# Keeping the attention output in SBUF between two stages of a transformer layer, and two block ends without GpSimd's drain

## Chip, cores and metric

One Trainium2 chip. The kernel runs on 8 cores, one sequence of the batch on each, with no exchange between them. Cores 0 to 3 lie on one die, 4 to 7 on the other. The metric is the device time of one execution in microseconds (us), that of the slowest core.

## The reference

A layer of a transformer, post-norm, for 8 sequences of 2048 tokens and width 2048. The attention is over features: the scores are a 2048 × 2048 matrix of feature against feature. The FFN has 8192 hidden units and ternary weights, which are made from the float weights inside the computation.

```python
q = einsum('bse,ef->bsf', x, Wq); k = ...Wk; v = ...Wv
scores = einsum('bes,bfs->bef', qT, kT) / sqrt(64)      # E x E per sequence
attn   = softmax(scores, axis=-1)
o      = einsum('bef,bfs->bes', attn, vT)               # E x S
x = layernorm(x + einsum('bse,ef->bsf', swap(o), Wo))
w_q = sign(w) * (abs(w) >= 0.7 * mean(abs(w)))          # for w1 and w2
h = gelu(einsum('bsd,fd->bsf', x, w1_q) + b1)
x = layernorm(x + einsum('bsf,df->bsd', h, w2_q) + b2)
```

## The kernel before

Sizes: P = 128 partitions, S = E = 2048 (16 row blocks each), FF = 8192 (64 row blocks). Every matmul takes a 128 × 128 left operand and 512 columns in bf16. Each stage is one block with a program for each engine, and a barrier of all engines stands at a block's end. A block has the drain of GpSimd in front of that barrier, unless it is made with `no_gpsimd_drain=True`. Here `p2`, `p3`, `f1`, `f2` are, `p1` and `p4` are not.

- **p1** (to about 928 us): mean of |w1| and |w2| on ScalarE; q, k, v on TensorE. q and v are spilled to `q_h` and `v_h` in HBM, k stays in `big1`. At the end GpSimd issues the loads of the first half of Wo into `wbuf` (two DMAs, which cast f32 to bf16); they are needed in `p4`.
- **p2** (to about 1226 us): first the thresholds on VectorE, a small matmul that spreads them (L484), then for each of 16 blocks the scores in `psS` from `qsl`, a slice loaded from `q_h` in pieces of 256 bytes, by SP, two blocks ahead. SP issues the first only when all q and v spills have landed. The softmax numerators go to `big0`, row block e at `big0[:, e*S : e*S+S]`, the reciprocals of the row sums to `recip_all`.
- **p3** (1226 to 1591 us): for each row block e_m TensorE transposes the 16 tiles of `big0` row block e_m into `psTA` or `psTB`, ScalarE copies them to `atsl` (L658), TensorE multiplies `atsl` by v in `big1` into `psO` (L635, 64 matmuls). ScalarE evacuates `psO` times the reciprocal to the staging tile `ostg` (L663), waits for that evacuation and stores it to `o_h` in HBM. `psO` and `atsl` exist once, so evacuation, copy and the next matmuls come one after the other. TensorE issues the transposes of the next row block ahead of the wait for the evacuation.
- **p4** (1591 to 2062 us): for each of 16 token blocks s_m SP loads `osl`, the columns of that block from all of `o_h`, again in pieces of 256 bytes, two buffers. TensorE makes the 128 × 2048 block of o·Wo (L749): 32 matmuls with `wbuf`, then 32 with `wobuf2`, the second half of Wo, which GpSimd loads at the stage's start. VectorE adds the residual `xres` to it in four pieces (L783) and, after ScalarE has made the statistics and the square root, applies the layer norm to `x2t` (L799). ScalarE casts to `x2b` (L857) and stores to `x2_h`. TensorE transposes `x2b` three blocks later into `psT4` (L732), and ScalarE copies this to `big0` (L812), column block pm of every row block: this is the left and moving side of the FFN. TensorE starts block s_m only when VectorE has done two pieces of the block before.
- **Quantizing** runs beside `p2`, `p3`, `p4` and `f1`: 256 tiles of w1 and w2, in pairs. GpSimd loads a pair to `qin` when VectorE is done with the pair before (`emit_quant_loads`, L216). VectorE makes two masks (L225, L228) and their difference in `qout` (L236), for which the spill of the pair before must have landed. SP spills a pair to `w1q_h` or `w2q_h` (`emit_quant_spills`, L208). `qin` and `qout` exist once, so a pair's round trip is a chain of a load, VectorE and a store. In `p4`, 3 tiles stand in VectorE's program in each token block, one before the statistics are waited for and two after. SP's program interleaves the spills with the `osl` loads; before `osl` of block s_m it waits for TensorE to finish block s_m − 2 (`t_y`).
- **f1** (2071 to 2963 us): h = gelu(x·w1), 64 row blocks of 64 matmuls (L911), weight slices `w1sl` loaded by SP from `w1q_h`; the 128 tiles of w2 are quantized beside it. **f2** (from 2963 us): h·w2, residual, layer norm, output.

Of the kernel before, what the change touches and what calls it, by code (L numbers as in the profile page):

```python
# [6 lines left out]
BF16 = mybir.dt.bfloat16  # L7
# [4 lines left out]
P = 128  # L12
S = 2048
E = 2048
# [64 lines left out]
def build_nc(upto=6, debug=False):  # L79
# [21 lines left out]
    o_h = nc.dram_tensor("o_h", [E, S], BF16, kind=scratch_kind)  # L101
# [8 lines left out]
    with contextlib.ExitStack() as stx:  # L110
# [66 lines left out]
        with nc.sbuf_tensor("big0", [P, nE * S], BF16) as big0, \  # L177
# [64 lines left out]
            with nc.sbuf_tensor("big1", [P, nE * S], BF16) as big1:  # L242

                with nc.psum_tensor("psA", [P, 2048], F32) as psA, \
# [3 lines left out]
                     nc.Block("p1") as blk:  # L248
# [348 lines left out]
                if upto >= 3:  # L597
                    with nc.psum_tensor("psO", [P, 2048], F32) as psO, \
# [3 lines left out]
                         nc.sbuf_tensor("ostg", [P, 2 * 2048], BF16) as ostg, \  # L602
# [48 lines left out]
                        def _(s):  # L651
                            s.wait_ge(v_rc.h, 16)
                            for e_m in range(nE):
# [7 lines left out]
                                if e_m >= 2:  # L661
                                    c_o.wait_item(s, e_m - 2)
                                s.activation(ostg[:, (e_m % 2) * 2048:  # L663
                                                  (e_m % 2) * 2048 + 2048],
# [4 lines left out]
                                s.wait_ge(a_oev.h, e_m + 1)  # L669
                                c_o.issue(s, hap(o_h, e_m * P * S, [[S, P], [1, S]]),  # L670
                                          ostg[:, (e_m % 2) * 2048:
                                               (e_m % 2) * 2048 + 2048])

            if upto >= 4:
                QT4_LO = QT_P2 + QT_P3
                with nc.psum_tensor("psy0", [P, 512], F32) as psy0, \
# [6 lines left out]
                     nc.sbuf_tensor("osl", [P, 2 * 2048], BF16) as osl, \  # L683
# [4 lines left out]
                     nc.Block("p4") as blk:  # L688
# [20 lines left out]
                    def _(sy):  # L709
                        c_o.wait_all(sy)  # L710
                        for s_m in range(nS):
                            if s_m >= 2:
                                sy.wait_ge(t_y.h, s_m - 1)
                            s_osl.issue(
                                sy, osl[:, (s_m % 2) * 2048:(s_m % 2) * 2048 + 2048],
                                hap(o_h, s_m * P, [[S, P], [P * S, nE], [1, P]]))
                            emit_quant_spills(
                                sy, QT4_LO + (s_m * (QT_W1 - QT4_LO)) // nS)
# [3 lines left out]
                    def _(t):  # L722
# [15 lines left out]
                        psy = [psy0, psy1, psy2, psy3, psy4, psy5]  # L738
                        for s_m in range(nS):
                            s_osl.wait_item(t, s_m)  # L740
                            if s_m >= 1:
                                t.wait_ge(v_z.h, max(0, 4 * s_m - 2))
                            for e_k in range(nE):
# [4 lines left out]
                                for nb in range(4):  # L748
                                    mm = t.matmul(  # L749
                                        psy[(4 * s_m + nb) % 6][:],  # L750
                                        osl[:, (s_m % 2) * 2048 + e_k * P:
                                            (s_m % 2) * 2048 + e_k * P + P],
# [52 lines left out]
                    def _(s):  # L805
# [4 lines left out]
                        def x2fm_evacs(pm):  # L810
                            s.wait_ge(t_tr4.h, pm + 1)
# [366 lines left out]
```

## Time and profile before

| | us |
|---|---|
| two runs | 3947.11 and 4346.39, median 4146.75 |
| the profiled execution | 3943.83 |
| span of its slowest core (core 1) | 3942.3 |
| spans of the 8 cores | 3898.1 to 3942.3 |
| granted TensorE clock, mean, each core | 0.925 to 0.927 |

The page of the profile, by engine and by slice of the span (40 slices, 98.6 us each; a digit is a busy share in tenths):

```profile
PE 3238.6 (82%) x14917; PEld 1457.3 (37%) x14917; DVE 1256.4 (32%) x1362; ACT 740.1 (19%) x1065; POOL 92.6 (2%) x166
PE   0986899835985877466649999999997999989997
DMA  9899966874345545566646777776656333372232
```

PE is TensorE, PEld its weight loads, DVE VectorE, ACT ScalarE, POOL GpSimd, SP SyncE; a q behind a name is the engine's own instruction queue, which issues DMAs. TensorE is the busiest by far, and its slices show where it isn't: `p1`'s start, its end (slice 9), and slices 16 to 20, which are the end of `p3` and `p4`. The idle time before an instruction stands in brackets in the timelines, with what ended it.

### The profile page before, as it was taken

What the parts mean: (1) busy time and instruction counts of PE and PEld (TensorE: products, weight loads), DVE (VectorE), ACT (ScalarE), POOL (GpSimd) and SP (SyncE); (2) the same over time, 40 slices, a digit from 0 to 9 for tenths busy, and PEclk for the clock granted to TensorE, in tenths of its full rate; (3) what the DMA queues carried; (4) which work ended last, traced back from release to release, by engine and by line L of the source; (5) the groups of instructions that cost most, each with busy time, mean ns of one, the idle gap of its engine ahead of it and who ended that gap; (6) DMA issues with size and microseconds to landing.
All of it is one profiled execution on the core that took longest, in us unless ns stands there. A gap on an engine that the chain in (4) does not pass through costs nothing. (4 is left out here: it accounts for less than half of the span.)

```text
span 3942.3 us, 37616 instructions; the slowest of 8 cores (3898.1 to 3942.3 us)
## 1 busy us (share of the span) xinstructions
PE 3238.6 (82%) x14917; PEld 1457.3 (37%) x14917; DVE 1256.4 (32%) x1362; ACT 740.1 (19%) x1065; POOL 92.6 (2%) x166
## 2 busy tenths in 40 slices
PE   0986899835985877466649999999997999989997
PEld 0432344312432333122224444444442444434443
DVE  0111211101443444144434334343431333323333
ACT  1344433340111111123331111111110000200002
POOL 0000000000000000000000000000000000000000
PEclk9998999967997989787779999999998999999998
DMA  9899966874345545566646777776656333372232
GB/s 186 214 249 252 241 171 176 231 218 94 100 111 177 164 155 157 126 203 202 192 155 182 187 187 187 187 203 190 194 171 218 128 128 115 132 244 81 112 128 86
DMA packets 392943, 673.62 MB, mean 171 GB/s; under 512 B 210432, under 2 KB 267840, under 8 KB 368192
## 3 DMA queue, kind: packets, MB, share of 16 engines
q1 hardware_dynamic: 291216, 377.55, 31.3%
q0 software_dynamic: 41648, 184.60, 19.8%
q10 hardware_dynamic: 59904, 109.06, 7.7%
q8 instruction: 119, 1.95, 0.2%
q14 instruction: 56, 0.46, 0.0%
HBM read 545.37 MB, written 159.38 MB: 179 GB/s over the span
## 5 line engine op out<-in xcount | busy, mean ns | idle before, releaser
L911 PE MATMUL psH<-big,w1sl 128*128 128x512 bf16 x4096 | 887.2, 379 | 14.0 <-DMA w1sl<-w1q_h 14.0
L1005 PE MATMUL psF<-w2g,hg 128*128 128x512 bf16 x4096 | 890.8, 380 | 0.0
L911 PEld LDWEIGHTS psH<-big,w1sl 128*128 128x128 bf16 x4096 | 400.4, 98 | 500.4 <-issue 20.7
L1005 PEld LDWEIGHTS psF<-w2g,hg 128*128 128x128 bf16 x4096 | 400.4, 98 | 490.1 <-issue 13.0
L225 DVE TENSOR_SCALAR qmask<-qin,tbc 128x1024 f32<-128x1024 f32 x256 | 208.0, 812 | 777.3 <-DMA qin<-w2t 475.5
L1055 DVE TENSOR_TENSOR oacc<-psF,oacc 128x2048 f32<-128x2048 f32 x112 | 256.6, 2292 | 583.1 <-PE psF L1005 583.1
L430 ACT ACTIVATE qmask<-sbin 128x1024 f32<-128x1024 f32 x256 | 270.3, 1056 | 484.1 <-DMA sbin<-w1t 212.7
L236 DVE TENSOR_TENSOR qout<-qmask 128x1024 bf16<-128x1024 f32 x256 | 313.7, 1226 | 135.2 <-DMA w1q_h<-qout 60.3
L635 PE MATMUL psO<-big,atsl 128*128 128x512 bf16 x1024 | 248.5, 408 | 91.8 <-ACT atsl L658 65.2
L299 PE MATMUL psA<-wbuf,big 128*128 128x512 bf16 x1024 | 228.7, 385 | 111.0 <-DMA wbuf<-wq 98.2
L299 PE MATMUL psB<-wbuf,big 128*128 128x512 bf16 x1024 | 231.4, 388 | 49.1 <-DVE spillb L345 49.1
L928 ACT ACTIVATE hstg<-psH,b1sb 128x2048 bf16<-128x2048 f32 x64 | 126.0, 1969 | 751.6 <-PE psH L911 751.6
L497 PE MATMUL psS<-big,qsl 128*128 128x512 bf16 x1024 | 231.5, 389 | 18.7 <-DMA qsl<-q_h 18.7
L749 PE MATMUL psy<-wbuf,osl 128*128 128x512 bf16 x512 | 133.8, 427 | 127.3 <-DMA osl<-o_h 113.2
L228 DVE TENSOR_SCALAR qmask<-qin,tbc 128x1024 f32<-128x1024 f32 x256 | 206.5, 807 | 0.0
L635 PEld LDWEIGHTS psO<-big,atsl 128*128 128x128 bf16 x1024 | 104.9, 104 | 230.3 <-issue 127.6
L299 PEld LDWEIGHTS psA<-wbuf,big 128*128 128x128 bf16 x1024 | 101.1, 99 | 236.1 <-issue 119.1
L314 PE MATMUL psA<-big,wbuf 128*128 128x512 bf16 x512 | 113.8, 384 | 74.9 <-ACT wbuf L409 74.9
L299 PEld LDWEIGHTS psB<-wbuf,big 128*128 128x128 bf16 x1024 | 101.7, 100 | 176.9 <-issue 61.8
L497 PEld LDWEIGHTS psS<-big,qsl 128*128 128x128 bf16 x1024 | 101.4, 100 | 148.3 <-issue 35.0
L749 PEld LDWEIGHTS psy<-wbuf,osl 128*128 128x128 bf16 x512 | 53.8, 107 | 204.1 <-issue 159.5
L314 PE MATMUL psB<-big,wbuf 128*128 128x512 bf16 x512 | 111.8, 379 | 6.7 <-ACT wbuf L409 6.7
(107 smaller groups left out, 1150.5 us busy)
## 6 DMA issues: line engine op xcount, KB each, us to landing
sbin<-w1t SPq DMA_DIRECT2D x128, 512.0 KB, 6.2
sbin<-w2t SPq DMA_DIRECT2D x128, 512.0 KB, 5.8
qin<-w1t POOLq DMA_DIRECT2D x64, 1024.0 KB, 6.3
qin<-w2t POOLq DMA_DIRECT2D x64, 1024.0 KB, 7.7
w2g<-w2q_h SPq DMA_DIRECT2D x16, 4096.0 KB, 14.1
w1q_h<-qout SPq DMA_DIRECT2D x64, 512.0 KB, 7.2
w1sl<-w1q_h SPq DMA_DIRECT2D x64, 512.0 KB, 10.7
w2q_h<-qout SPq DMA_DIRECT2D x64, 512.0 KB, 9.0
```

The costliest lines, as they stand in the source:

```text
L225: v.tensor_scalar(qmask[:], src, tbc[:, 4 * j:4 * j + 1], tbc[:, 4 * j + 1:4 * j + 2], op0=ALU.subtract, op1=ALU.is_ge)
L228: v.tensor_scalar(qmask2[:], src, tbc[:, 4 * j + 2:4 * j + 3], tbc[:, 4 * j + 3:4 * j + 4], op0=ALU.subtract, op1=ALU.is_le).then_inc(g_qm ...
L236: v.tensor_tensor(qout[:, (i % 2) * 1024:(i % 2) * 1024 + 1024], qmask[:], qmask2[:], op=ALU.subtract).then_inc(v_qt.h, 1)
L299: mm = t.matmul(pv, big0[:, e_k * S + s_m * P:e_k * S + s_m * P + P], half[:, e_k * 512:e_k * 512 + 512], start=(e_k == 0), stop=(e_k == n ...
L314: mm = t.matmul(ps[:, sn * 512:sn * 512 + 512], wbuf[:, (f_m % 8) * 2048 + e_k * P: (f_m % 8) * 2048 + e_k * P + P], big0[:, e_k * S + sn ...
L430: s.activation(sink[:], sbin[:, (i % 3) * 1024:(i % 3) * 1024 + 1024], AF.Abs, accum_out=stats_acc[:, i:i + 1]).then_inc(a_st.h, 1)
L497: mm = t.matmul(ps[:, nb * 512:nb * 512 + 512], qsl[:, (e % 2) * 2048 + s_k * P: (e % 2) * 2048 + s_k * P + P], big1[:, s_k * S + nb * 512 ...
L635: mm = t.matmul(psO[:, sn * 512:sn * 512 + 512], atsl[:, f_k * P:f_k * P + P], big1[:, f_k * S + sn * 512: f_k * S + sn * 512 + 512], star ...
L749: mm = t.matmul(psy[(4 * s_m + nb) % 6][:], osl[:, (s_m % 2) * 2048 + e_k * P: (s_m % 2) * 2048 + e_k * P + P], wsrc[:, wof + nb * 512:wof ...
L911: mm = t.matmul(ps[:, nb * 512:nb * 512 + 512], w1sl[:, (f_m % 2) * 2048 + d_k * P: (f_m % 2) * 2048 + d_k * P + P], big0[:, d_k * S + nb ...
L1005: mm = t.matmul(ps[:, nb * 512:nb * 512 + 512], hg[:, slot * 8192 + f_k * 1024 + j * P: slot * 8192 + f_k * 1024 + j * P + P], w2g[:, slot ...
L1055: v.tensor_tensor(oacc[:, j * 2048:j * 2048 + 2048], ps[:], oacc[:, j * 2048:j * 2048 + 2048], op=ALU.add).then_inc(v_fa.h, 1)
```

## The change

Four edits, of which two belong together:

1. `p3` writes the evacuated attention output over `big0`, row block e_m, whose transposes have been read by then, instead of to `ostg`. The store to `o_h`, the wait ahead of it and the tensor `o_h` go. A wait of ScalarE for the transposes of its own row block is added.
2. `p4` takes its left operand from `big0` at `big0[:, e_k*S + s_m*P : +P]`. The `osl` loads and their waits go, as does SP's wait on `t_y` that paced them. TensorE waits once for the last evacuation of `p3`. ScalarE's copy L812, which writes into the same columns, gets a wait for TensorE to be done with that token block.
3. `p1` and 4. `p4` are made with `no_gpsimd_drain=True`.

```diff
-                     nc.Block("p1") as blk:
+                     nc.Block("p1", no_gpsimd_drain=True) as blk:
...
                                 s.wait_ge(t_o.h, e_m + 1)
-                                if e_m >= 2:
-                                    c_o.wait_item(s, e_m - 2)
-                                s.activation(ostg[:, (e_m % 2) * 2048:
-                                                  (e_m % 2) * 2048 + 2048],
+                                s.wait_ge(t_tr.h, e_m + 1)
+                                s.activation(big0[:, e_m * S:e_m * S + S],
                                              psO[:], AF.Copy,
                                              scale=recip_all[:, e_m:e_m + 1]
                                              ).then_inc(a_oev.h, 1)
                                 a_oev.inc(1)
-                                s.wait_ge(a_oev.h, e_m + 1)
-                                c_o.issue(s, hap(o_h, e_m * P * S, [[S, P], [1, S]]),
-                                          ostg[:, (e_m % 2) * 2048:
-                                               (e_m % 2) * 2048 + 2048])
...
-                     nc.Block("p4") as blk:
+                     nc.Block("p4", no_gpsimd_drain=True) as blk:
...
                     def _(sy):
-                        c_o.wait_all(sy)
                         for s_m in range(nS):
-                            if s_m >= 2:
-                                sy.wait_ge(t_y.h, s_m - 1)
-                            s_osl.issue(
-                                sy, osl[:, (s_m % 2) * 2048:(s_m % 2) * 2048 + 2048],
-                                hap(o_h, s_m * P, [[S, P], [P * S, nE], [1, P]]))
                             emit_quant_spills(
                                 sy, QT4_LO + (s_m * (QT_W1 - QT4_LO)) // nS)
...
+                        t.wait_ge(a_oev.h, nE)
                         for s_m in range(nS):
-                            s_osl.wait_item(t, s_m)
                             if s_m >= 1:
                                 t.wait_ge(v_z.h, max(0, 4 * s_m - 2))
...
                                         psy[(4 * s_m + nb) % 6][:],
-                                        osl[:, (s_m % 2) * 2048 + e_k * P:
-                                            (s_m % 2) * 2048 + e_k * P + P],
+                                        big0[:, e_k * S + s_m * P:e_k * S + s_m * P + P],
...
                             s.wait_ge(t_tr4.h, pm + 1)
+                            s.wait_ge(t_y.h, pm + 1)
                             s.copy(bass.AP(big0, pm * P, [[nE * S, P], [S, nE], [1, P]]),
```

## Rows read from the trace of the kernel before

**Rows 1.** The page of the profile, its first line.

```profile
span 3942.3 us, 37616 instructions; the slowest of 8 cores (3898.1 to 3942.3 us)
```

**Rows 2.** Busy time by stretch (p4's middle, f1); then clock, DMA share, GB/s.

```profile
1722.00:1824.00 102.00, 66.63 (x320) 31.19 (x320) 48.14 (x77) 32.80 (x60) 5.25 (x10) 0.80 0.63 196
...
2071.00:2963.00 892.00, 886.72 (x4096) 400.27 (x4094) 353.08 (x384) 125.34 (x64) 33.31 (x63) 1.00 0.67 186
```

**Rows 3.** Groups of instructions, 1592 to 2062 us: busy, mean ns | idle before, releasers.

```profile
L749 PE MATMUL psy<-wbuf,osl 128*128 128x512 bf16 x512 | 133.8, 427 | 127.3 <-DMA osl<-o_h 113.2 <-DVE x2t L783 14.1
```

**Rows 4.** Timeline around the end of p1: start, duration, instructions [idle before].

```profile
911.37 14.14 ACTq L58 DMA_DIRECT2D v_h<-spillb  x2
...
923.20 1.49 POOL L58 DMA_DIRECT2D wbuf<-wo  x2 [415.43 <-PE psB L314]
...
954.04 0.36 DVE L512 TENSOR_SCALAR thw<-tvals 1x1 f32<-1x1 f32 x2 [26.65 <-PEq L248]
...
966.30 44.04 PE L497 MATMUL psS<-big,qsl 128*128 128x512 bf16 x191
```

**Rows 5.** DMA issues at p1's end and p2's start: count, KB, us to landing.

```profile
wbuf<-wo POOLq DMA_DIRECT2D x1, 2048.0 KB, 29.4
...
v_h<-spillb ACTq DMA_DIRECT2D x1, 512.0 KB, 9.8
...
qsl<-q_h SPq DMA_DIRECT2D x3, 512.0 KB, 4.8
```

**Rows 6.** Timeline of p3, one row block; the last row is from p1.

```profile
1298.07 1.97 ACT L663 ACTIVATE ostg<-psO,recip_all 128x2048 bf16<-128x2048 f32 x1 [16.39 <-PE psO L635]
...
1300.59 1.87 ACT L658 COPY atsl<-psTA 128x2048 bf16<-128x2048 bf16 x1 [0.55 <-ACT ostg L663]
...
1303.17 15.45 PE L635 MATMUL psO<-big,atsl 128*128 128x512 bf16 x64 [4.30 <-ACT atsl L658]
...
272.49 15.38 PE L299 MATMUL psB<-wbuf,big 128*128 128x512 bf16 x64 [3.02 <-DVE spillb L345]
```

**Rows 7.** DMAs at p4's start: issue, landing times, and queues from 1600 to 1630.

```profile
1592.36 1.55 POOL L58 DMA_DIRECT2D wobuf<-wo  x2
...
wobuf<-wo POOLq DMA_DIRECT2D x1, 2048.0 KB, 30.3
...
osl<-o_h SPq DMA_DIRECT2D x1, 512.0 KB, 39.0
...
q0 software_dynamic: 1273, 6.45, 93.6%
q1 hardware_dynamic: 1381, 0.35, 7.4%
```

**Rows 8.** Timeline of p4's start.

```profile
1632.54 9.40 PE L749 MATMUL psy<-wbuf,osl 128*128 128x512 bf16 x32 [44.11 <-DMA osl<-o_h]
...
1649.04 0.69 DVE L783 SCALAR_TENSOR_TENSOR x2t<-psy,xres 128x512 f32<-128x512 f32 x1 [73.45 <-PE psy L749]
```

**Rows 9.** Timeline of p4, two token blocks (a cycle).

```profile
1720.73 0.69 DVE L783 SCALAR_TENSOR_TENSOR x2t<-psy,xres 128x512 f32<-128x512 f32 x1 [5.63 <-PE psy L749]
...
1752.53 1.23 DVE L236 TENSOR_TENSOR qout<-qmask 128x1024 bf16<-128x1024 f32 x1 [4.68 <-DMA w1q_h<-qout]
...
1754.86 9.67 PE L749 MATMUL psy<-wbuf,osl 128*128 128x512 bf16 x32 [8.60 <-DMA osl<-o_h]
...
1771.82 0.69 DVE L783 SCALAR_TENSOR_TENSOR x2t<-psy,xres 128x512 f32<-128x512 f32 x1 [5.06 <-PE psy L749]
```

**Rows 10.** Landing of a spill in that cycle, with and without an osl load beside it.

```profile
w1q_h<-qout SPq DMA_DIRECT2D x1, 512.0 KB, 13.2
...
w1q_h<-qout SPq DMA_DIRECT2D x1, 512.0 KB, 8.6
```

**Rows 11.** The chain of work in f1, two spills in a row: start, duration.

```profile
2102.14 9.15 DMA w2q_h<-qout
...
2115.72 8.36 DMA w2q_h<-qout
```

More of the change, by code:

```diff
@@ L100, in build_nc @@
     v_h = nc.dram_tensor("v_h", [E, S], BF16, kind=scratch_kind)
-    o_h = nc.dram_tensor("o_h", [E, S], BF16, kind=scratch_kind)
     x2_h = nc.dram_tensor("x2_h", [S, E], F32, kind=scratch_kind)
@@ L601, in build_nc @@
                          nc.sbuf_tensor("atsl", [P, 2048], BF16) as atsl, \
-                         nc.sbuf_tensor("ostg", [P, 2 * 2048], BF16) as ostg, \
                          nc.Block("p3", no_gpsimd_drain=True) as blk:
@@ L682, in build_nc @@
                      nc.psum_tensor("psT4", [P, 2048], BF16) as psT4, \
-                     nc.sbuf_tensor("osl", [P, 2 * 2048], BF16) as osl, \
                      nc.sbuf_tensor("xres", [P, 2 * 2048], F32) as xres, \
```

## The prediction

> **What bounds the kernel now.** I read first the busy time by stage, then what ended the idle time of TensorE in the stages that the diff touches, then those stretches in order of time. The profiled execution spans 3942.3 us [rows 1] and took 3943.8 us as a whole; the sum below is made against 3943.8. The median of the two runs shown (4146.75) is the mean of 3947.11 and 4346.39. The profiled time agrees with the lower one within 0.1%, so I forecast against that level.
>
> The last two stages (`f1`, `f2`, from 2071 on) hold nearly half of the time and nothing in the diff enters them. In `f1` TensorE is busy 886.7 of 892 us [rows 2]. They will move as a block, earlier by what the stages before them give. In `p4` TensorE is far from full: its 512 matmuls on the first half of Wo alone waited 113.2 us for `osl<-o_h`, the tile that the change abolishes, against 14.1 us for VectorE [rows 3]. 44.1 us of that is one wait [rows 8] at the start of `p4`; the other 69.1 us are seven waits, one in every second row block from the third on. The question is what each of these waits hides. What removing a wait is worth is what comes second, not the wait.
>
> **Part 1, the block end of `p1`.** GpSimd issues the two Wo loads at 923.20. VectorE is then idle 26.65 us until 954.04, at the block's end barrier [rows 4]. The second, issued about 923.95, lands 29.4 us later [rows 5], at 953.3, 0.7 us ahead of the release. So I read the 26 us as the drain waiting for these loads, and with `no_gpsimd_drain` the barrier opens at about 928.5. It is not all gained: the loads still have to land, and three things come between.
> - SP waits for the last `v_h` spill. The last store of the two, issued about 925.2, lands 9.8 us later [rows 4, 5], so the first `qsl` load can't leave before 935.
> - The threshold chain on VectorE and the small matmul behind it take 966.3 − 954.0 = 12.3 us [rows 4] and would be over at 941, so they are no longer last.
> - `qsl` then shares the DMA engines with Wo. A `qsl` load takes 4.8 us alone [rows 5]. The nearest row for it in competition is the first `osl` load, of the same shape and also right behind two Wo loads: it landed 39.0 us after issue, while the second Wo load had landed at 1593.14 + 30.3 = 1623.4 and `osl` only at 1632.5 [rows 7, 8].
>
> Bounds: if the engines gave `qsl` half of their time, it would land at 935.3 + 2 × 4.8 = 945, a gain of 966.3 − 945 = 21. If all that is queued goes ahead (Wo until 953.3, two `qsl` loads 9.6, the first `qin` 3 to 5), it lands at 966 to 968, a gain of nothing or a loss of 2. I take a landing 8 us behind Wo, about what `osl` shows: 961, **a gain of 5**.
>
> The Trainium skill, DMA: Bandwidth & Descriptors, section on queues, rings and completion order, says that an engine takes turns between its queues packet by packet. The rows agree: from 1600 to 1630 SP's queue moved 1381 packets beside 1273 of GpSimd's [rows 7], which is turn by turn. By that rule `qsl` (2048 small packets) can't be through before Wo's remaining 4 KB packets are, so about 957 would be its earliest, a gain of at most 9.
>
> The same flag on `p4` I cost at nothing: GpSimd's last load there landed long before the last piece of ScalarE work.
>
> **Part 2, the loop of `p3`.** For each of the 16 row blocks ScalarE evacuates `psO`, waits for its own evacuation, issues the `o_h` store, then copies the next transposed tile, and TensorE waits for that copy (4.30 us of idle time) [rows 6]. Evacuation to copy takes 1300.59 − 1298.07 = 2.52 us, of which 1.97 is the evacuation and 0.55 idle [rows 6]. The destination changes from `ostg` to `big0`, with the same shape and type, so 1.97 stays; the new wait on `t_tr` was met before the copy and costs nothing. The 0.55 to 0.65 go, 15 times on the path (the last is the next part's): **a gain of 9**, bounds 7 and 10. The 16 stores are off TensorE's path here, and I count no more for them. TensorE's gap shrinks to 3.7 us, which won't spare its slow start: after a gap of 3.02 us 64 matmuls took 15.38 us [rows 6], as after 4.30.
>
> **Part 3, the start of `p4`.** Before, TensorE waits 44.11 us for `osl` and starts at 1632.54; the first residual add is at 1649.04 [rows 8]. After, the left operand is already in `big0`, so the first 32 matmuls start at once, and then wait for the second half of Wo (`wobuf2`). This is the new wait. It landed at 1623.4. Without `osl` beside it, it should land earlier by its share: SP's queue held 7.4% of the engines [rows 7], 2.2 of 30 us, and 0.4 us come from the store no longer issued, so 1620.8. The 32 matmuls behind it take 9.4 us with a slow start, as the first 32 do now [rows 8], and the add starts at 1630.3: **a gain of 19**. Bounds: 16 if the landing doesn't move, 21 if it moves by a whole `osl` load.
>
> **Part 4, the steady part of `p4`.** Two row blocks take 1771.82 − 1720.73 = 51.1 us [rows 9], a cycle that repeats six times after it has begun. In one block of the two the `osl` load leaves together with `qin`, `xres`, the `x2_h` store and the spill of quantized weights. There the spill lands 13.2 us after its issue, in the other block 8.6 [rows 10]. This delays two chains:
> - TensorE starts at 1754.86 after 8.60 us of waiting for `osl` [rows 9], so it could start at 1746.3, held there by the transposes. It then ends at 1762.8 instead of 1771.4.
> - VectorE, quantizing in between, writes at 1752.53 after waiting 4.68 us for the spill [rows 9]. The pieces behind that leave it free 5.06 us before the next add at 1771.82 [rows 9], at 1766.7. So even with an unchanged spill the cycle gives 5.1.
>
> Without `osl` the burst loses 4.8 of about 15 us of DMA work. Between 8.6 and 13.2 I take 10.0 for the spill, the lower end plus a bit for the `x2_h` store that the other block doesn't have. VectorE is then free 3.2 us earlier, at 1763.5, or 1763.1 with `qin` a little faster too. So both chains meet at about 1763, and the new bound is the quantizing chain on VectorE and its two DMAs: 8.7 us per cycle. There are seven such waits: 7 × 8.7 = **a gain of 61**. Bounds: 7 × 5.1 = 36 with the spill at 13.2, and 7 × 9.2 = 65 with it at 8.6, where TensorE is last. SP's spills no longer stand behind the `t_y` wait; this gives nothing, since they were issued right after their tile. DMA share is 0.63 here [rows 2], so bandwidth isn't the next bound. The added `t_y` wait of ScalarE is met a few row blocks before: zero.
>
> **Sum.** 5 + 9 + 19 + 61 = 94, and 3943.8 − 94 = **3850 us**, 2.4% less.
>
> **Rivals.**
> - *The spill stays slow* (13 us because of `qin`, `xres` and `x2_h`, not of `osl`). For it speaks that three megabyte-sized transfers stay in that burst; against it that the other block lands in 8.6 with two of them. It gives 5 + 9 + 19 + 36 = 69: 3875 us. Chance 0.17.
> - *Everything at the good end*: `qsl` gets through early, the latencies of all DMAs in `p4` fall. 21 + 10 + 21 + 65 = 117: 3827 us. Against it stands the late `osl` landing. Chance 0.08.
> - *Slower: quantizing takes over `f1`.* There each pair of tiles goes round in 2115.72 − 2102.14 = 13.6 us [rows 11], while TensorE needs 892/64 = 13.9 per slice; the weights for the next stages come from that loop, and the spills share SP's queue with TensorE's `w1sl` loads. If the pair grows by 1.8 us it adds 64 × 1.5 = 96 us and the whole gain is gone; at 3.0 us more it adds 173 and the kernel is at 4023. Against it: nothing in `f1` is changed, and its DMA traffic stays. Chance 0.04.
> - *The flag doesn't lift the 26 us*, because the barrier waits for something else. It costs only the 5 of part 1: 3855, within the forecast's own range.
>
> **Chances and range.** The forecast has 0.71, with its own range of 3833 to 3873. 2% of the time, about what a measurement can tell from no change, is 79 us, so the boundary lies at 3865, between the forecast and the first rival. Of the forecast's 0.71 I put 0.05 above the boundary, where the spill is between 11 and 13. Faster: 0.66 + 0.08 = 0.74. Within 2%: 0.17 + 0.05 = 0.22. Slower: 0.04. The range for 8 in 10 takes in the upper half of the good rival and the first rival with a little spread: 3820 to 3880.
>
> **What would show it.** Part 1: after the last `p1` work, SP and VectorE resume within 1 us, and the first L497 matmul is at 957 to 966 in the old time. Part 2: ScalarE's copy follows the evacuation without the 0.55 us, and TensorE's gap is 3.7. Part 3: TensorE starts at the block's start, then waits some 15 us for `wobuf<-wo`. Part 4: no `osl`; two row blocks take 42 to 43 us, with idle time of VectorE on `qin` and the spill as the largest rest. `f1` keeps its 892 us, and `f1` and `f2` together their 3942 − 2071 = 1871. The forecast is wrong if the cycle stays above 46 us (the spill), or `f1` gets longer by more than 10 us.

## The result, and the profile after

The changed kernel takes 0.9774 of the time of the kernel before, with a 95% interval of 0.9749 to 0.9799: 2.3% less. Its lowest execution took 3849.17 us (before: 3944.47 in the same session), and the profiled one 3859.17 (before: 3943.83). Executions of either kernel in which the cores of a die show a lower granted clock take 4 to 12% longer (one of the two runs behind the median of 4146.75 is such a one), so everything below compares undisturbed executions or, where a profile shows one die disturbed, cores 4 to 7 of the other.

The page of the kernel after (the span of its slowest core, core 2, then busy time, then slices as before):

```profile
span 3857.6 us, 37557 instructions; the slowest of 8 cores (3821.2 to 3857.6 us)
PE 3236.5 (84%) x14917; PEld 1456.7 (38%) x14917; DVE 1255.9 (33%) x1362; ACT 736.9 (19%) x1065; POOL 92.6 (2%) x166
PE   0987899926984888677759999999988999989997
DMA  9899965875345444555647766777547233462232
```

TensorE is busy for as long as before; only idle time has gone. Where, a table by stretch shows. Each number is worked out from the first and last starts of one line's instructions on each core, as the mean of the eight cores (L635 is the matmul of `p3`, in the kernel after at L633):

| stretch, us | before | after | difference | forecast |
|---|---|---|---|---|
| start to the last value matmul of `p1` | 918.5 | 920.2 | +1.7 | 0 |
| from there to the first score matmul | 43.6 | 37.2 | −6.4 | −5 |
| `p2`, first to last score matmul | 247.7 | 248.4 | +0.7 | 0 |
| from there to the first matmul of `p3` | 44.6 | 45.1 | +0.5 | 0 |
| `p3`, first to last L635 | 327.7 | 315.3 | −12.4 | −9 |
| from there to the first residual add of `p4` | 59.2 | 39.5 | −19.7 | −19 |
| `p4`, first to last residual add | 377.8 | 333.2 | −44.6 | −61 |
| from there to `f1` | 41.5 | 40.8 | −0.7 | 0 |
| `f1`, first to last matmul | 887.5 | 888.6 | +1.1 | 0 |
| from there to the end | 975.8 | 974.1 | −1.7 | 0 |

Together −81.5 us in the mean span of the cores in these two profiled executions (3923.9 to 3842.4), where the forecast's parts add up to −94. The ratio of all undisturbed executions, which takes the slowest core of each, makes it 89. Three of the four parts came out within 4 us. The steady part of `p4` gave 45 and not 61.

**The end of `p1`.** Timeline of the kernel after, its slowest core; it answers to [rows 4]:

```profile
920.82 1.49 POOL L58 DMA_DIRECT2D wbuf<-wo  x2 [417.91 <-PE psB L313]
...
925.44 0.15 ACT L445 COPY tvals<-psA 1x4 f32<-1x4 f32 x1 [27.86 <-PE psA L324]
...
933.63 41.15 SPq L58 DMA_DIRECT2D qsl<-q_h  x3
...
937.83 0.56 PE L483 MATMUL psS<-tq,ones_f 1*128 1x8 f32 x2 [12.48 <-DVE thw L550]
...
958.36 41.88 PE L496 MATMUL psS<-big,qsl 128*128 128x512 bf16 x184 [19.96 <-DMA qsl<-q_h]
```

The barrier is open at once: VectorE goes on at 926, SP issues at 933.63, when the last v spill has landed, and the threshold chain is over at 938. Then TensorE waits 19.96 us for `qsl`. The two DMAs, by the time from issue to landing:

```profile
wbuf<-wo POOLq DMA_DIRECT2D x1, 2048.0 KB, 32.3
...
qsl<-q_h SPq DMA_DIRECT2D x1, 512.0 KB, 24.6
```

The second Wo load lands at about 921.6 + 32.3 = 953.9 (29.4 us after issue before, [rows 5], now slowed by `qsl`), and `qsl` at 958.2, 4 us behind it.

**`p3`.** Timeline from one row block into the next, to be read beside [rows 6]:

```profile
1295.78 15.66 PE L633 MATMUL psO<-big,atsl 128*128 128x512 bf16 x64 [3.66 <-ACT atsl L656]
...
1311.60 1.97 ACT L660 ACTIVATE big<-psO,recip_all 128x2048 bf16<-128x2048 f32 x1 [16.49 <-PE psO L633]
1313.46 1.86 ACT L656 COPY atsl<-psTB 128x2048 bf16<-128x2048 bf16 x1
...
1316.03 13.97 PE L633 MATMUL psO<-big,atsl 128*128 128x512 bf16 x64 [3.69 <-ACT atsl L656]
```

Evacuation to copy takes 1.86 us instead of 2.52, and the gap is 3.7 us, as forecast. What the forecast excluded is the last row: in 2 of the 15 row blocks that follow a gap (3 on two of the eight cores) the 64 matmuls took 13.97 us, with no slow start. The granted clock was 1.00 in the first 3 us of that block and 0.69 in those of the block at 1295.78.

**The start of `p4`**, beside [rows 7, 8]:

```profile
1577.44 8.44 PE L734 MATMUL psy<-wbuf,big 128*128 128x512 bf16 x32 [6.33 <-DMA b2bf<-b]
1604.73 8.45 PE L734 MATMUL psy<-wobuf,big 128*128 128x512 bf16 x32 [18.85 <-DMA wobuf<-wo]
1613.38 0.69 DVE L767 SCALAR_TENSOR_TENSOR x2t<-psy,xres 128x512 f32<-128x512 f32 x1 [53.19 <-PE psy L734]
```

The new wait is where it was expected, for the second half of Wo. A small one for `b2bf` stands before it and costs nothing behind the larger one. On the mean of the eight cores (below: the mean core) the second load of `wobuf` lands 25.5 us after its issue, where it took 28.0 beside `osl`.

**The steady part of `p4`**, one cycle of two token blocks, beside [rows 9]: VectorE's tile behind a spill, TensorE's first half, VectorE's first residual add.

```profile
1736.00 1.23 DVE L235 TENSOR_TENSOR qout<-qmask 128x1024 bf16<-128x1024 f32 x1 [2.46 <-DMA w1q_h<-qout]
...
1743.32 0.69 DVE L767 SCALAR_TENSOR_TENSOR x2t<-psy,xres 128x512 f32<-128x512 f32 x1 [1.79 <-PE psy L734]
...
1752.08 1.23 DVE L235 TENSOR_TENSOR qout<-qmask 128x1024 bf16<-128x1024 f32 x1 [4.73 <-DMA w1q_h<-qout]
...
1765.59 0.69 DVE L767 SCALAR_TENSOR_TENSOR x2t<-psy,xres 128x512 f32<-128x512 f32 x1
...
1787.39 0.69 DVE L767 SCALAR_TENSOR_TENSOR x2t<-psy,xres 128x512 f32<-128x512 f32 x1 [1.83 <-PE psy L734]
```

The cycle is 1787.39 − 1743.32 = 44.1 us where I had 42.4 and the kernel before 51.1. The `osl` waits are gone and VectorE's wait for the spill is as long as it was (4.73 against 4.68 us). The same holds for the whole steady part, here on core 2 (what waited for what, us in total, times, the longest):

```profile
DVE qmask L224 <- DMA qin<-w1t: 58.8, 18, 5.2
...
DVE qout L235 <- DMA w1q_h<-qout: 53.2, 19, 5.1
```

On the mean core VectorE waits there 64 us for loads of tiles, 51 for spills and 5 for TensorE; before it was 89, 51 and 32. So VectorE and the DMAs of its tiles are what `p4` waits for now, as the prediction said they would be.

The landing times of that spill and its neighbour, beside [rows 10]:

```profile
w1q_h<-qout SPq DMA_DIRECT2D x1, 512.0 KB, 11.6
...
w1q_h<-qout SPq DMA_DIRECT2D x1, 512.0 KB, 8.7
```

### The profile page after: what moved, and what is told of

Read it like the earlier page. It is cut to its first block and busy times, and to the rows that moved or that the text cites. A ratio compares the mean times of both kernels' runs of the same rounds, so it can differ in the third digit from the quotient of the medians.

```text
span 3857.6 us, 37557 instructions; the slowest of 8 cores (3821.2 to 3857.6 us)
## 1 busy us (share of the span) xinstructions
PE 3236.5 (84%) x14917; PEld 1456.7 (38%) x14917; DVE 1255.9 (33%) x1362; ACT 736.9 (19%) x1065; POOL 92.6 (2%) x166
## 5 line engine op out<-in xcount | busy, mean ns | idle before, releaser
L633 PE MATMUL psO<-big,atsl 128*128 128x512 bf16 x1024 | 247.7, 407 | 83.7 <-ACT atsl L656 55.3
L496 PE MATMUL psS<-big,qsl 128*128 128x512 bf16 x1024 | 228.2, 385 | 41.5 <-DMA qsl<-q_h 41.5
L633 PEld LDWEIGHTS psO<-big,atsl 128*128 128x128 bf16 x1024 | 105.0, 104 | 221.4 <-issue 118.2
L734 PE MATMUL psy<-wbuf,big 128*128 128x512 bf16 x512 | 130.1, 418 | 25.2 <-DVE x2t L767 18.9
L734 PE MATMUL psy<-wobuf,big 128*128 128x512 bf16 x512 | 114.5, 382 | 18.8 <-DMA wobuf<-wo 18.8
```

What stands on the lines that cost most here:

```text
L496: mm = t.matmul(ps[:, nb * 512:nb * 512 + 512], qsl[:, (e % 2) * 2048 + s_k * P: (e % 2) * 2048 + s_k * P + P], big1[:, s_k * S + nb * 512 ...
L633: mm = t.matmul(psO[:, sn * 512:sn * 512 + 512], atsl[:, f_k * P:f_k * P + P], big1[:, f_k * S + sn * 512: f_k * S + sn * 512 + 512], star ...
L734: mm = t.matmul(psy[(4 * s_m + nb) % 6][:], big0[:, e_k * S + s_m * P:e_k * S + s_m * P + P], wsrc[:, wof + nb * 512:wof + nb * 512 + 512] ...
```

## The experiments

All times by stretch are as in the table above, and "steady part" is the first to the last residual add of `p4`.

### 1. The flag of p1 alone

```diff
 # the kernel before
-                     nc.Block("p1") as blk:
+                     nc.Block("p1", no_gpsimd_drain=True) as blk:
```

> The kernel before with one edit: the block p1 is made without GpSimd's drain. Theory (the barrier waited for the two Wo loads, and what the barrier gives back is mostly lost to the same loads, which now run beside the first q slice): SP and VectorE go on within 1 us of the end of p1's work, the first score matmul starts about 37 us after the last matmul of p1's values instead of 43.6 (mean of the cores), the rest is unchanged, 3938 us, within 2%. Rival 1, the barrier waits for something else: the 43.6 us stay. Rival 2, the early start brings nothing at all: the stretch stays 43.6 although the barrier opens early. Both rivals: 3944 us.

Measured on cores 4 to 7: from the last value matmul to the first score matmul 36.2 us (before: 43.4). The barrier, in the timeline of core 5:

```profile
920.63 1.49 POOL L58 DMA_DIRECT2D wbuf<-wo  x2 [417.15 <-PE psB L314]
922.62 0.33 ACTq L58 DMA_DIRECT2D v_h<-spillb  x1
925.84 0.36 DVE L512 TENSOR_SCALAR thw<-tvals 1x1 f32<-1x1 f32 x2 [1.02 <-PEq L248]
```

VectorE goes on after 1.02 us, where it waited 26.65 [rows 4]. So the drain was the wait, and 7 us of the 26 are what one gets for it. That the drain waited for the Wo loads, the kernel before shows core by core: the second load lands 29.8 to 31.2 us after the last value matmul, and on each of the eight cores VectorE goes on 0.7 us behind that landing. As a whole no difference from the kernel before could be told by time alone.

### 2. The output in big0, with both drains back

```diff
 # the kernel after
-                     nc.Block("p1", no_gpsimd_drain=True) as blk:
+                     nc.Block("p1") as blk:
...
-                     nc.Block("p4", no_gpsimd_drain=True) as blk:
+                     nc.Block("p4") as blk:
```

> The changed kernel with the drain of GpSimd back at the ends of p1 and p4, so only the attention output stays in big0. Theory (three gains by place: 12 us in p3, 20 at the start of p4, 45 in its steady part, nothing at the end of p4): 3857 + 6 = 3863 us, about 2.1% less than before, the stretch from the last residual add of p4 to the first FFN matmul is 41 us with or without the drain. Rival (the flag at the end of p4 has a part in the gain): that stretch is longer by more than 2 us than in the changed kernel.

Measured: the end of `p1` is back at 43.5 us on cores 4 to 7, `p3` 315.6, steady part 333.3, and from the last add to `f1` 40.4 (after: 40.9). The flag on `p4` does nothing there. The gain of the rest hardly depends on the flags: only the first residual add of `p4` comes 1.7 us later after `p3` (41.6 against 39.9 us), with the second load of `wobuf` landing later.

### 3. The stores back in p3

```diff
 # the kernel after, p3, ScalarE, behind the evacuation
                                 a_oev.inc(1)
+                                s.wait_ge(a_oev.h, e_m + 1)
+                                c_o.issue(s, hap(o_h, e_m * P * S, [[S, P], [1, S]]),
+                                          big0[:, e_m * S:e_m * S + S])
```

> The changed kernel with the 16 stores of the attention output to o_h put back into p3, from big0, and ScalarE's wait for its own evacuation ahead of each; nothing reads o_h. The prediction had 0.6 us for each of 15 row blocks in p3 (9 us), the changed kernel showed 12.4. Theory 1 (wait and issue on ScalarE are all of it): the p3 stretch goes back from 315 to 327 us, p4 stays at 333 between its first and last residual add. Theory 2 (the rest of the 12.4 is less DMA traffic for the load of the values and for quantizing): the same, since the traffic is back as well, but then the first p3 matmul moves too. Rival (p3's gain came from the wait for the landing of older stores): the stretch stays near 318.

Measured on cores 4 to 7: `p3` 328.7 us (before 327.8, after 315.5), steady part 333.0. The whole gain of `p3` is the store with ScalarE's wait and issue; where the store reads from plays no part. The run puts the wait and the stores' DMA traffic back together and doesn't separate them. Two things speak for the wait: TensorE's gap is 4.3 us again where it was 3.7, and the first matmul of `p3`, which the second theory had move, doesn't come later (43.1 us after the last of `p2`, against 45.2). The evacuations in the kernel after come 20.2 us apart, and 18.5 in two or three of fifteen cases; before and here mostly 20.5 to 20.9, with one or two of 22. The forecast 9 is in the shorter gap, and two spared slow starts of 1.7 us make up the rest.

### 4. The osl traffic back, without its wait

```diff
 # the kernel after, p4, SyncE
                         for s_m in range(nS):
+                            if s_m >= 2:
+                                sy.wait_ge(t_y.h, s_m - 1)
+                                s_osl.wait_item(sy, s_m - 2)
+                            s_osl.issue(
+                                sy, osl[:, (s_m % 2) * 2048:(s_m % 2) * 2048 + 2048],
+                                hap(q_h, s_m * P, [[E, P], [P * E, nE], [1, P]]))
                             emit_quant_spills(
```

> The changed kernel with the 16 loads of 256-byte pieces put back on SP in p4 at their old places and with their old pacing, into a tile that nothing reads (they read q_h, which lies the same way as o_h did). TensorE waits for none of them. It tells the wait from the traffic. Theory (mine: without the traffic the spill of quantized weights lands in 10 instead of 13 us, which is a good part of the gain in p4): the steady part of p4 grows from 333 to about 350 us, and the first residual add moves 2 us later. Rival (the wait of TensorE was all that counted): 333 stays. Rival 2 (the pacing and the issue on SP's queue hold up the spills): over 360.

Measured: steady part 344.5 us over all cores (345.7 on cores 4 to 7), against 333.2 without the traffic and 377.8 with traffic and wait. So of the 44.6 us some 11 are traffic that spills and loads no longer share, and 33 are TensorE's wait. The rival that only the wait counts falls, and my price of the traffic (17) was too high. The first residual add comes 4 us later, not 2. The slow spill of each cycle shows why the traffic matters less than I had it: it lands in 12.7 to 13.2 us before (core 1), in 11.5 to 12.0 after and in 11.2 to 12.8 here (core 2).

### 5. The transposes in the middle of the next block

```diff
 # the kernel after, p4, TensorE
                                 if s_m == 0 and e_k == 8:
                                     g_wo2.wait_all(t)
+                                if s_m >= 4 and e_k == 8:
+                                    x2_transposes(s_m - 4)
...
-                            if s_m >= 3:
-                                x2_transposes(s_m - 3)
+                        x2_transposes(nS - 4)
                         x2_transposes(nS - 3)
```

> The changed kernel, in p4 the 16 transposes of an older token block are issued after the first 32 matmuls of the next block instead of ahead of them. In the changed kernel the blocks of p4 last 21.5 and 22.5 us in turn. Theory (the short one, which I had forecast at 19.6, is ended by a chain: layer norm, ScalarE's cast, its copy of psT4, the transposes that wait for it, then 64 matmuls with a slow start; the long one by the quantizing chain on VectorE): the short block falls to 19.6 to 20, the long one stays, so the steady part goes from 333 to about 320 us. Rival (both blocks are held by the quantizing chain): 333 stays. Rival 2 (the matmuls' own length decides): 333 stays too, with TensorE busy all through the block.

Measured: steady part 333.5 us, unchanged (ratio 0.9789, interval 0.9768 to 0.9810). The short block did as the theory said, but the sum is that of the first rival. The first residual adds of three token blocks in a row, on core 2:

```profile
1762.42 0.68 DVE L768 SCALAR_TENSOR_TENSOR x2t<-psy,xres 128x512 f32<-128x512 f32 x1
...
1782.27 0.68 DVE L768 SCALAR_TENSOR_TENSOR x2t<-psy,xres 128x512 f32<-128x512 f32 x1
...
1806.94 0.68 DVE L768 SCALAR_TENSOR_TENSOR x2t<-psy,xres 128x512 f32<-128x512 f32 x1
```

The short block is 19.8 us, as the theory had it, and the long one has grown to 24.7. Their sum is 44.5, as before the edit. Over the eight cores the seven long blocks grew by 8.0 us together and the eight others shrank by 7.7. TensorE waits for nothing but VectorE's residual adds in the steady part:

```profile
PE psy L736 <- DVE x2t L768: 84.6, 15, 11.1
```

VectorE in turn waits 0.1 us for TensorE on the mean core, 71 for loads of tiles and 51 for spills. So the quantizing chain sets the sum of two blocks, in which three pairs of tiles are quantized. The prediction's way of adding up the ends of single blocks falls here.

### 6. Two pairs of quantized tiles

```diff
 # the kernel after
-             nc.sbuf_tensor("qout", [P, 2 * 1024], BF16) as qout, \
+             nc.sbuf_tensor("qout", [P, 4 * 1024], BF16) as qout, \
...
-                    if i >= 2:
-                        c_wq.wait_item(v, i // 2 - 1)
+                    if i >= 4:
+                        c_wq.wait_item(v, i // 2 - 2)
```

> The changed kernel with room for two pairs of quantized tiles in qout, so a pair no longer waits for the landing of the spill just ahead of it, only for the one before that (the statistics buffers of p1 lie over it, for room). Theory (the long block of p4 is ended by the spill, which lands 11.6 to 12.0 us after its issue where I had forecast 10): the long block falls from 22.5 to about 20, the short one stays at 21.5, the steady part goes from 333 to about 315 us. Rival (the load of the next pair decides, the spill only came last by a hair): less than 5 us of gain. f1 stays at 886.

Measured: steady part 310.5 us, 23 less, and 0.972 of the kernel before (interval 0.9694 to 0.9746). VectorE in the same place, core 2:

```profile
1725.25 0.69 DVE L773 SCALAR_TENSOR_TENSOR x2t<-psy,xres 128x512 f32<-128x512 f32 x1 [3.35 <-PE psy L740]
...
1734.47 1.23 DVE L236 TENSOR_TENSOR qout<-qmask 128x1024 bf16<-128x1024 f32 x1 [0.17 <-DVE qmask L228]
1741.55 0.81 DVE L225 TENSOR_SCALAR qmask<-qin,tbc 128x1024 f32<-128x1024 f32 x1 [5.85 <-DMA qin<-w1t]
```

No wait for a spill is left on any core; the load of the next pair is what VectorE waits for now (67 us on the mean core). The tiles and their traffic are the same, so this is what the wait for the spill cost, and the rival of less than 5 us falls. The token blocks are 20.7 us on average.

### 7. Sixteen tiles moved from p4 to p2

```diff
 # the kernel after
-QT_P2 = 24
+QT_P2 = 40
```

> The changed kernel with 40 instead of 24 of the 256 tiles quantized in p2, so 32 instead of 48 are left for p4: two in each token block, one pair. Theory (the quantizing chain ends the long blocks of p4): without the long chain every block is ended by the transposes' chain or shorter, 20 us, and the steady part goes from 333 to about 305 us; p2 has 1.25 pairs of 11.7 us in each 14 us of matmuls, and its q loads stand behind the spills on SP, so it grows by 10 to 20 us. Sum: 3840 to 3850 us. Rival (p2 is ended by its spills from then on): p2 grows by more than p4 gives.

Measured: 0.9705 of the kernel before (interval 0.9674 to 0.9736). Its lowest execution took 3819.31 us, less than the 3840 to 3850 expected. Steady part 244.5 us, 89 less; `p2` 297.9, 50 more and not 10 to 20. The steady part fell much below the 305 that I expected, since with one pair in each block the round trip of 14 to 15 us fits inside what TensorE needs. TensorE in `p4`, on core 7:

```profile
1763.59 7.07 PE L734 MATMUL psy<-wbuf,big 128*128 128x512 bf16 x32
1770.50 7.07 PE L734 MATMUL psy<-wobuf,big 128*128 128x512 bf16 x32
1778.69 1.05 PE L717 MATMUL psT<-ident_bf,x2b 128*128 128x128 bf16 x16 [1.12 <-ACT big L797]
1779.58 7.07 PE L734 MATMUL psy<-wbuf,big 128*128 128x512 bf16 x32
```

Most blocks take 15.8 to 16.6 us, on average 16.3, and 64 matmuls take 14 us as at the full clock. VectorE now waits 50 us for TensorE and 1 for loads of tiles. So what bounds `p4` in the changed kernel isn't the transposes' chain but 1.5 round trips per block. The edit takes a third of the tiles' DMA traffic and of VectorE's work on them out of `p4` as well; of the 89 us, only the 23 of experiment 6 are shown with work and traffic unchanged.

The 50 us in `p2` are TensorE's waits for `qsl`, 56.5 us on the mean core where they were 19.6, and slower matmuls behind those gaps, 13 us. Lines of core 0:

```profile
1094.36 11.85 SPq L58 DMA_DIRECT2D w1q_h<-qout  x2
...
1106.30 0.39 SPq L58 DMA_DIRECT2D qsl<-q_h  x1
...
1115.03 15.15 PE L496 MATMUL psS<-big,qsl 128*128 128x512 bf16 x57 [10.12 <-DMA qsl<-q_h]
```

The load leaves right behind the second of two spills, which SP holds back until VectorE has made its tiles. So it is for all 14 later loads on all eight cores: each is issued 0.4 us behind a spill, on average 10.6 us after its buffer has come free (4.3 in the kernel after), and lands in 9.0 us (8.0). So, as far as the trace tells, it is the order on SP that costs the time, and the shared engines 1 us of each load. The expectation's rival holds as to the cause, but `p2` grew by less than `p4` gave.

### 8. The copy to atsl in halves

```diff
 # the kernel after, p3: ScalarE, then TensorE
-                                s.copy(atsl[:], pt[:]).then_inc(a_trs.h, 1)
+                                for hh in range(2):
+                                    s.copy(atsl[:, hh * 1024:hh * 1024 + 1024],
+                                           pt[:, hh * 1024:hh * 1024 + 1024]
+                                           ).then_inc(a_trs.h, 1)
...
-                                t.wait_ge(a_trs.h, e_m + 1)
+                                t.wait_ge(a_trs.h, 2 * e_m + 1)
...
+                                    if f_k == 8:
+                                        t.wait_ge(a_trs.h, 2 * e_m + 2)
```

> The changed kernel, in p3 ScalarE copies the transposed tiles to atsl in two halves, and TensorE starts after the first. Its gap in each of 15 row blocks should fall from 3.7 to 2.8 us. In the changed kernel two of the fifteen gaps of 3.69 us were followed by 64 matmuls in 13.97 us and the others by 15.66. Theory 1 (a gap under 3 us keeps the TensorE clock at 2.4 GHz, as 2.44 us did in p1): 15 x (0.9 + 1.7) = 39 us off the row blocks, but the quantizing of 28 pairs in p3 is over only 13 us before the stage's end and takes over, so the stage gives about 13 us and then stands. Rival (the clock falls all the same): 15 x 0.9 = 13 us, with 64 matmuls in 15.4 us.

Measured: 0.9759 of the kernel before (interval 0.9736 to 0.9783), so 6 us less than after by these ratios, whose intervals overlap, and 10 by the stretches of `p3` and its end. Three row blocks of `p3` on TensorE:

```profile
1349.69 13.97 PE L635 MATMUL psO<-big,atsl 128*128 128x512 bf16 x64 [2.84 <-ACT atsl L659]
...
1367.46 15.66 PE L635 MATMUL psO<-big,atsl 128*128 128x512 bf16 x64 [2.90 <-ACT atsl L659]
...
1386.82 13.97 PE L635 MATMUL psO<-big,atsl 128*128 128x512 bf16 x64 [2.81 <-ACT atsl L659]
```

With gaps of 2.8 to 2.9 us 9 or 10 of 15 row blocks on each core start at the full clock, where with 3.7 us it was 2 or 3. In the first 3 us of the three blocks above the granted clock was 1.00, 0.62 and 1.00. So neither the theory (all of them) nor the rival (none) holds. `p3` falls from 315 to 290 us, but from its last matmul to the first of `p4` it takes 20.6 instead of 6.1 us: the barrier waits for the quantizing of `p3`'s 28 pairs. As in `p4`, quantizing takes over.

### 9. Both quantizing edits together

```diff
 # the kernel after: QT_P2 = 40, and qout with two pairs as in experiment 6
```

> The two edits of qout_two_pairs and qt_p2_40 together: a second pair of qout, and 40 tiles quantized in p2. Theory (a pair's round trip, load, VectorE and spill, is what p4 and the longer p2 wait for, and both edits act on it): p4's steady part stays at the floor of 244 us that TensorE sets, p2 falls from 298 towards 280, since the spill leaves the round trip but the load stays; 3800 us. Rival (p2's 50 us came from the q loads behind the spills on SP): p2 stays at 298.

Measured: 0.9683 (0.9665 to 0.9701), the lowest execution 3803.35 us. `p2` 294.7 us instead of 297.9, steady part 240. The landing of the spill was not what held `p2`; taking it out of the round trip gave 3 us there and not the 18 that I expected. The rival holds: the loads of `qsl` still leave 0.4 us behind a spill, 10.4 us after their buffer has come free.

### 10. Loads and spills both off the round trip

```diff
 # the kernel of experiment 9, with the halves of experiment 8, and
-             nc.sbuf_tensor("qin", [P, 2 * 1024], F32) as qin, \
-             nc.sbuf_tensor("qmask", [P, 1024], F32) as qmask, \
-             nc.sbuf_tensor("qmask2", [P, 1024], F32) as qmask2, \
+             nc.sbuf_tensor("qin", [P, 4 * 1024], F32) as qin, \
+             nc.sbuf_tensor("qmask", [P, 2048], BF16) as qmask, \
...
-                    if p >= 1:
-                        g.wait_ge(g_qm.h, 2 * p)
+                    if p >= 2:
+                        g.wait_ge(g_qm.h, 2 * (p - 1))
```

> Two pairs of qin and of qout, masks in bf16 (for room), 40 tiles in p2, and the copy to atsl in halves. Theory (with loads and spills both off the round trip, VectorE's own 4 to 6 us per pair are left, and each stage falls to what TensorE sets): p2 250 to 260, p3 290 and no wait at its end (6 instead of 20 us), p4 244. Sum against the changed kernel: 5 more in p2, 25 less in p3, 89 less in p4: 3857 - 109 = 3748 us. Rival (the DMA engines, not the round trip, are full in p2): p2 over 275. f1 keeps 886, since TensorE is full there.

Measured: 0.9567 (0.9548 to 0.9585). `p3` 290.3 us with 6.0 at its end, steady part 240.8, `p2` 266.8. The expected sum was 3748; its lowest execution took 3757.42. `p2` stayed 7 to 17 us above what I expected, and 18 above the kernel after. On the mean core 10 of the 18 are TensorE's waits for `qsl` (29.6 us, 19.6 after) and 6.5 slower matmuls behind them. It is SP's order again: each load leaves 0.4 us behind a spill, 7.0 us after its buffer has come free, and lands in 8.9 us, as in experiments 7 and 9. An edit of that order was not tried.

### 11. The first half of Wo loaded in p3

```diff
 # the kernel of experiment 10, GpSimd
-                        g.wait_ge(t_q.h, 144)
-                        for j in range(2):
-                            g_wo.issue(
...
+                            for j in range(2):
+                                emit_quant_loads(g, QT_P2 + 16 * j, QT_P2 + 16 * j + 16)
+                                g_wo.issue(
```

> The kernel of quant_pipelined with the loads of the first half of Wo moved from the end of p1 into p3. In the changed kernel the first score matmul comes 37 us after the last value matmul, waiting 20 us for its q slice, which shares the engines with Wo. Theory (that contention is all that is left of the 26 us that the drain cost): the stretch falls from 37 to about 19, where the last v spill and the threshold chain end, and p3 doesn't grow by more than 2 us: another 16 us less. Rival (the q loads wait for something else): 37 stays.

Measured: 0.952 of the kernel before (interval 0.9495 to 0.9545). The stretch at `p1`'s end is 18.5 us (40.2 in the kernel of experiment 10), and `p3` stays at 290.0. The timeline:

```profile
919.27 1.79 SPq L58 DMA_DIRECT2D qsl<-q_h  x2
...
930.97 0.56 PE L484 MATMUL psS<-tq,ones_f 1*128 1x8 f32 x2 [12.47 <-DVE thw L551]
931.47 18.77 PE L497 MATMUL psS<-big,qsl 128*128 128x512 bf16 x78
```

Without Wo beside them the v spill lands 5.6 us after the last value matmul (12.6 in the kernel of experiment 10) and `qsl` comes in time, and the threshold chain is last, as the prediction's second bullet on part 1 had it without the loads. This kernel beats both others: 4.8% less than before, 2.6% less than after.

## Why the prediction was right or wrong

**The level and the sum.** I set the sum against 3943.8 and left the median of 4146.75 beside it. The forecast of 3850 is 2.4% below the one and 7% below the other, and the change gives 2.3%. The prediction had only the distance of the two runs to go by and should have given its difference as a ratio. That the sum came so near is in part luck: parts 1 to 3 gave 5.5 us more than forecast and part 4 gave 16 less.

**Part 1: right in mechanism and size.** The barrier waited for the Wo loads (experiment 1: 26.65 to 1.02 us), and most of the time came back as a wait for `qsl`, landing at 958.2, 4 us behind Wo where I took 8. Forecast 5, measured 6.4. From the Trainium skill, DMA: Bandwidth & Descriptors, section on queues, rings and completion order (an engine takes turns between its queues, packet by packet), the prediction had estimated 957 as the earliest landing. The trace is near it: from the issue of `qsl` until Wo had landed, SP's queue moved 602 packets beside 774 of GpSimd's, so most of the 2048 small packets of `qsl` came behind Wo, and it landed at 958.2. That it was the contention, experiment 11 shows: 18.5 us with Wo out of the way.

**Part 2: right in mechanism, too small.** The 0.65 us per row block and the gap of 3.7 us are as said. The step that failed here is "which won't spare its slow start": two of fifteen were spared, 3.4 us of the 12.4. I had one row (3.02 us, slow) and took it for a bound, where experiment 8 shows both outcomes at 2.8 us.

**Part 3: right**, 19.7 against 19, the new wait for `wobuf` included. On the mean core that load lands 2.5 us sooner after its issue, where 2.2 were forecast, and the 32 matmuls behind it take 9.2 us to the add, where 9.4 were.

**Part 4: right in mechanism, 61 forecast, 44.6 measured.** This is the step of the prediction that failed, a term of the sum that was mis-sized: "Between 8.6 and 13.2 I take 10.0 for the spill", with the other block of the cycle left as it was. On the mean core the seven long blocks gave 50.5 us, not 61, and the eight others took 5.9 back:
- *The spill's landing.* I took 10.0 us, near the row of the other block; it is 11.5 to 12.0. Of the 4.6 us that it lay above the other block's, `osl` was 1 to 1.5; the rest stayed with the `x2_h` store, `xres` and `qin` still in that burst (which of them holds it was not tried). Experiment 4 prices the `osl` traffic at 11 us for the whole part, where my step from 13.2 to 10.0 was worth (8.7 − 5.1) × 7 = 25 against the first rival; the rival (36 in place of 61) was nearer than the forecast. The forecast also stood at the end of its own range: in the cycle that it read, TensorE could start 8.60 us earlier, so 8.7 needed both chains at their best, and the 9.2 of the upper bound doesn't follow from TensorE.
- *The block that I left alone.* I had the other block at 19.6 us unchanged. It is 21.3 to 21.8, ended by TensorE behind ScalarE's copy. Experiment 5 shows that mending it alone gives nothing: with it back at 19.8 the other grows by as much.
- *The method.* Both come from adding the ends of single blocks. What repeats is the round trip of a pair, one and a half times in each block: 44.1/3 = 14.7 us after, where 42.4/3 = 14.1 was forecast. (Before, 51.1/3 = 17.0 had TensorE's wait for `osl` in it.) Experiments 6 and 7 show it from both sides: the wait for the spill out of the round trip gives 23 us, and one pair per block instead of one and a half gives 89, down to where VectorE waits for TensorE.
- *The core.* I read core 1 and multiplied by seven. On the mean core the steady part was 377.8 us before and on core 4 only 365.7, since its cycles were 49 us and not 51.

**f1 and f2** stayed within 2 us of before. The rival that quantizing takes over `f1` didn't come about, but quantizing was what bounded `p4` after, and the end of `p3` in experiment 8.

## What to carry to other kernels

When a wait is removed, look for the loop that runs beside the one you are reading, and price it by its own period: here a load, a short piece of VectorE and a store on single buffers, three times in two blocks. In `p4` one pair less in every second block gave 89 us, where taking away the round trip through HBM had given 45. But then follow the loop's own queue: the tiles moved to `p2` cost 50 us there, since SP issues TensorE's loads behind the spills of tiles. A drain that seems to cost 26 us may be a wait for loads that the next stage then shares the engines with; move the loads too (7 us without the drain, 22 more with the loads moved as well, from 40.2 to 18.5).

## What the runs showed of the hardware

- Whether a gap on TensorE costs a slow start isn't decided by its length alone in the range seen here. After gaps of 2.8 to 2.9 us the first matmuls ran at 2.4 GHz (granted clock 1.00) in 9 or 10 of 15 cases on each core, after 3.7 us in 2 or 3, after 4.3 us and more in none. A slow start (granted clock 0.62 to 0.69 in the first 3 us) cost 1.7 us for 64 matmuls.
- A q slice of 512 KB in 256-byte pieces landed 24.6 us after its issue beside 4 MB (as written) of Wo, and 4.8 us without; the issue of the next one held SP's queue for 18 to 20 us there, and for 22 to 29 us at the start of `p4` in the kernel before.
- With the quantizing masks in bf16 instead of f32 (experiment 11) the difference of the two masks took 0.69 us instead of 1.23, 256 times, and VectorE's busy time over the kernel fell from 1255.9 to 1120.9 us.
- While both queues had work at the start of `p4` before (1600 to 1623.4 us), SP's queue moved 915 packets of 256 bytes and GpSimd's 918, most of 4 KB: turn by turn, with 7.2% and 93.1% of the engines' time.
- The drain of GpSimd at a block's end opened the barrier 0.7 us behind the landing of GpSimd's last load, on each of eight cores; at the end of `p4`, where GpSimd's last load had landed long before, it cost nothing that the stretches show (40.4 against 40.9 us).
